# A graph layer with routed experts on one core: smaller late blocks of tokens, their weights copied by ACT, and four places for their buffers

## What is computed

```python
# x: 10000 x 128, adj: 10000 x 10000, float32
h = item_feat @ W_item.T + b_item
x = x + relu(adj @ h + layernorm(x) @ W_user.T + b_user)
xf = layernorm(x)
probs = softmax(xf @ gate_w + gate_b)          # 8 experts
vals, idx = top_k(probs, 2)                    # cw: the two weights of each token
for e in range(8):                             # W1: 128 x 256, W2: 256 x 128
    out += cw[:, e] * (gelu(xf @ W1[e] + b1[e]) @ W2[e] + b2[e])
x = x + out
```

## Time and profile before

| | us |
|---|---|
| median of three runs | 1801.21 (1801.1 to 1806.88) |
| the profiled execution | 1804.49 |
| its span, first to last instruction | 1802.7 |
| busy in it: PE, DVE, ACT, POOL | 1463.0, 1289.1, 1058.1, 822.6 |
| granted TensorE clock, mean | 0.906 of full |

### The profile page before, as it was taken

One profiled execution on the slowest core, in us unless ns is written; L12 is line 12 of the kernel. 1 busy time (PEld: TensorE's weight loads), 2 busy tenths in 40 slices (PEclk: granted clock), 3 DMA queues, 4 the chain that ended last, 5 costly groups with the idle time before them and its releaser, 6 DMA issues. The chain is left out here.

```text
span 1802.7 us, 23294 instructions
## 1 busy us (share of the span) xinstructions
PE 1463.0 (81%) x6505; PEld 1186.0 (66%) x6505; DVE 1289.1 (72%) x2462; ACT 1058.1 (59%) x1227; POOL 822.6 (46%) x507
## 2 busy tenths in 40 slices
PE   7999999999898989889898898989889873544340
PEld 6877777877776768677776777767777652433330
DVE  6988888898787778778787787877888763422220
ACT  5766767676675767567676676766767642322220
POOL 2013221331736346273653736437264465566565
PEclk9999999999999989899999999999999985766665
DMA  9999999998989888898998989989899953222222
GB/s 356 337 326 342 333 321 356 338 352 293 299 269 303 267 284 279 274 304 282 296 301 279 299 281 303 296 288 293 274 311 292 293 165 84 50 37 37 34 25 21
DMA packets 226520, 458.52 MB, mean 254 GB/s; under 512 B 78410, under 2 KB 113335, under 8 KB 226333
## 3 DMA queue, kind: packets, MB, share of 16 engines
q1 hardware_dynamic: 123942, 425.69, 68.5%
q0 software_dynamic: 92144, 27.11, 10.4%
q10 hardware_dynamic: 10390, 5.25, 1.0%
HBM read 429.03 MB, written 31.13 MB: 255 GB/s over the span
## 5 line engine op out<-in xcount | busy, mean ns | idle before, releaser
L681 DVE TENSOR_TENSOR a_lo<-raw,a_hi 128x1000 fp32r<-128x1000 f32 (+1 forms) x800 | 927.1, 1185 | 164.1 <-ACT a_hi L539 157.5
L539 ACT ACTIVATE a_hi<-raw 128x1000 fp32r<-128x1000 f32 (+1 forms) x800 | 812.1, 1027 | 339.8 <-PE acc L950 173.6
L948 PE MATMUL acc<-a_hi,h_hi 128*128 128x500 f32 x1580 | 657.5, 416 | 58.4 <-DVE a_lo L681 42.4
L950 PE MATMUL acc<-a_hi,h_lo 128*128 128x500 f32 x1580 | 624.3, 395 | 0.0
L949 PE MATMUL acc<-a_lo,h_hi 128*128 128x500 f32 x1580 | 624.2, 395 | 0.0
L477 POOL DMA_INDIRECT out<-yr_sb,tok_at x156 | 364.1, 2334 | 380.2 <-DVE yr_sb L851 330.7
L948 PEld LDWEIGHTS acc<-a_hi,h_hi 128*128 128x128 f32 x1580 | 305.6, 193 | 158.2 <-DVE a_lo L681 96.3
L950 PEld LDWEIGHTS acc<-a_hi,h_lo 128*128 128x128 f32 x1580 | 303.9, 192 | 63.1
L949 PEld LDWEIGHTS acc<-a_lo,h_hi 128*128 128x128 f32 x1580 | 306.0, 194 | 55.7 <-issue 4.6
L457 POOL DMA_INDIRECT lists<-rows_sb,dest_at x160 | 238.5, 1490 | 137.5 <-issue 66.9
L444 POOL TENSOR_TENSOR rstd_sb<-var_sb,power_sb 125x4 f32<-125x4 f32 x20 | 38.2, 1909 | 271.7 <-DVE var_sb L704 271.7
(11 more groups left out here) (160 smaller groups left out, 1358.7 us busy)
## 6 DMA issues: line engine op xcount, KB each, us to landing
raw<-in_adj_main SPq DMA_DIRECT2D x780, 500.0 KB, 6.0
xg_sb<-lists SPq DMA_DIRECT2D x39, 273.4 KB
xr_sb<-in_xR SPq DMA_DIRECT2D x20, 250.0 KB
out<-x_sb ACTq DMA_DIRECT2D x20, 250.0 KB
items<-in_itemT SPq DMA_DIRECT2D x13, 384.0 KB, 8.7
lists<-rows_sb,dest_at POOLq DMA_INDIRECT x160
out<-yr_sb,tok_at POOLq DMA_INDIRECT x156, 8.1
lists<-in_filling SPq DMA_DIRECT2D x8, 273.4 KB, 3.9
```

Source lines behind the costliest of these rows:

```text
L539: nc.scalar.activation(a_hi[q][0:rows, 0:cols], raw[s][0:rows, 0:cols], ACT.Copy).then_inc(hi_ready, 1)
L681: nc.vector.tensor_tensor(a_lo[s][0:rows, 0:cols], raw[s][0:rows, 0:cols], val(a_hi[q][0:rows, 0:cols]), ALU.subtract).then_inc(lo_ready, 1)
L948: nc.tensor.matmul(acc[:, 0:T], w_hi, m_hi, start=(k == 0), stop=False)
L950: last = nc.tensor.matmul(acc[:, 0:T], w_lo, m_hi, start=False, stop=(k == KT))
```

## The change

Blocks ahead of the late ones are 31 rather than 30: three (`EARLY`) run beside the tail of the last tile, which is walked over 52 positions rather than 40. Late blocks have 4, 2 or 1 parts of 125 rows, by `late_blocks`: a block may have u parts while the waiting rows are certain to fill it in at least one list. With 4500 rows waiting this gives 4, 4, then seven times 2, then twenty-one times 1, 30 blocks with 43 parts. Row counts in `picked` and in the loads are in rows and not in blocks. Filler is 125 rows rather than 500 for each list. ACT copies the late blocks' weights (`copy_expert`) into one of three places; GpSimd copies only those of the first 31. `picked`, `one_hot` and the scaled rows have four places. GpSimd's order has `tail` ahead of the add of the block before, in every pass. In DVE's late loop pick comes first and the meta last. A few positions in the passes move by one: the second load (19 to 20), `keep` (22 to 23 and 34 to 35), `to_rows` (24 to 25, 36 to 37).

```diff
 PER = 2
 FIRST = 6
+EARLY = 3
 LOOPED = PER * (NB - FIRST)
+NLATE = LOOPED + EARLY
+def full(units):
+    return E * (units * TQ - 1) + 1
-WAITING = 2 * N - T * (LOOPED + PER)
-LATE = E + (WAITING - E) // T
-BLOCKS = LOOPED + PER + LATE
-NLATE = LOOPED + PER
+def late_blocks(waiting):
+    found = []
+    for units in (Q, 2, 1):
+        while waiting >= full(units):
+            found.append(units)
+            waiting -= units * TQ
+    return found + [1] * (E + (waiting - E) // TQ)
+LATE = late_blocks(2 * N - T * NLATE)
+BLOCKS = NLATE + len(LATE)
...
+def w_slot(n):
+    return n % 2 if n < NLATE else (n - NLATE + 1) % 3
...
+        added_rows = [yr_sb, raw[3], raw[6], raw[7]]
+        experts = [(w_block[s][:, 0, :], w_block[s][:, 1, :]) for s in range(2)] + [(a_hi[2][:, 0:WW], a_hi[3][:, 0:WW])]
...
-                sp.dma_start(lists[bass.ds(at, T), :], filling).then_inc(ends_filled, 16)
+                sp.dma_start(lists[bass.ds(at, TQ), :], filling[0:TQ, :]).then_inc(ends_filled, 16)
...
-            for i in range(FIRST, NB + 1):
+            for i in range(FIRST, NB):
                 n = PER * (i - FIRST)
                 weights(n)
+                tail(i)
                 if n:
                     add(n - 1, i - 2)
-                tail(i)
-                if i < NB:
-                    user(i)
+                user(i)
                 weights(n + 1)
                 add(n, i - 1)
                 dispatch(i)
...
             for n in range(NLATE, BLOCKS):
-                if n + 3 < BLOCKS:
-                    weights(n + 3)
                 add(n, NB)
...
+            def copy_expert(n):
+                act.wait_ge(picked_ready, n + 1)
+                at = act.value_load(picked[slot(n)][0:1, 1:2], min_val=0, max_val=E - 1)
+                act.wait_ge(down_done, n + 1 - w_reuse(n))
+                act.wait_ge(y_kept, n + 1 - w_reuse(n))
+                for half in range(2):
+                    nc.scalar.activation(experts[w_slot(n)][half], w_table[:, half, bass.ds(at * WW, WW)], ACT.Copy).then_inc(w_parted, 1)
+                nc.scalar.activation(b_block[w_slot(n)][:, :], bias_sb[:, bass.ds(at * NBIAS, NBIAS)], ACT.Copy).then_inc(w_parted, 1)
...
+            late_pick(NLATE)
+            late_pick(NLATE + 1)
+            for n in range(NLATE - 1, BLOCKS + 2):
+                if NLATE + 2 <= n + 3 < BLOCKS:
+                    late_pick(n + 3)
+                if NLATE <= n + 1 < BLOCKS:
+                    split_rows(numbered(n + 1), work(n + 1), units(n + 1))
+                if NLATE <= n < BLOCKS:
+                    split_g(numbered(n), work(n), units(n))
+                if NLATE <= n - 2 < BLOCKS:
+                    scale(numbered(n - 2), added_rows[yr_slot(n - 2)], slot(n - 2), 16 * units_before(n - 1 - yr_reuse(n - 2)), units(n - 2))
+                if NLATE <= n + 1 < BLOCKS:
+                    read_meta(numbered(n + 1), work(n + 1), slot(n + 1), (n + 1) % 2,
+                              16 * units_before(n + 2 - slot_reuse(n + 1)), units(n + 1))
```

More of the change, by code:

```diff
@@ L63 @@
 CAP = N + T
-SPARE = E * CAP // T
+SPARE = E * CAP
 WW = 2 * H
@@ L322, in build @@
         w_copied = sem("w_copied")
+        w_parted = sem("w_parted")
         meta_step = sem("meta_step")
@@ L426, in _ @@
             for n in range(NLATE, BLOCKS):
-                load_block(numbered(n), n % 2, work(n)["rows"], reuse(n), 16 * 2 * Q * NB)
+                load_block(n, NB)
         @block.gpsimd
@@ L598, in blocks @@
[L598 to L608 removed]
+                nc.scalar.activation(w["y"][:, 0:wide(u)], ps_y[:, 0:wide(u)], ACT.Identity,
+                                     bias=b_block[ws][:, HH:HH + 1]).then_inc(y_kept, 1)
@@ new lines, in blocks @@
+            def blocks(i, p, per):
+                w = works[0]
+                for s in range(per):
+                    at = p - s * APART
+                    if at == B_HI:
+                        split_rows(in_pass(i, s), w, 1, Q)
+                    if at == B_GELU:
+                        gelu(in_pass(i, s), w, 1, s % 2, Q)
+                    if at == B_GHI:
+                        split_g(in_pass(i, s), w, 1, Q)
+                    if at == B_KEEP:
+                        keep(in_pass(i, s), w, 1, s % 2, Q)
@@ L887, in _ @@
                 one_pass(i, True, True)
-            for p in range(NPOS):
+            for p in range(NPOS + APART):
+                blocks(NB, p, EARLY)
                 tail(NB, p)
@@ L1015, in down @@
-            def down(count, w, s):
+                    w_hi, w_lo = (half[:, j * P:(j + 1) * P] for half in expert)
+                    z = ps_z[j][:, 0:wide(u)]
+                    nc.tensor.matmul(z, w_hi, x_hi, start=True, stop=False)
+                    nc.tensor.matmul(z, w_hi, x_lo, start=False, stop=False)
+                    nc.tensor.matmul(z, w_lo, x_hi, start=False, stop=True).then_inc(z_done, 1)
+            def down(count, w, expert, u):
                 since(pe, y_kept, count(1, 0))
+                y = ps_y[:, 0:wide(u)]
```

331 lines of the change are left out of this document (163 added, 168 removed).

## The result

The changed kernel took 1754.03 us (median, 1749.78 to 1756.46) against 1801.15 of the kernel before beside it: a ratio of 0.973, 95% interval 0.9701 to 0.9758. The forecast was 1768, 33 us less; 47 came. The profiled execution has a span of 1751.3 us (before 1802.7), so the two spans differ by 51.4, and they are what the steps are read from.

A forecast was written before the change was run, and what follows sets the result against it. The 250 us end was taken as bound by a chain of adds and landings, not an engine's work. First late add 1562.9 + links 202.5 + end 7.1 - passes 3 = 1769.5 span, 1768 as median; range 1740 to 1790.

The forecast's parts named there:

- The late links: Chain of adds of the late blocks: 202.5 us from first late add to last, against 234.1 + 6.9 before.
- four places take VectorE's 3.1 us out of the link: Late blocks: with four places, VectorE needs only the add of four blocks ago, so its 3.1 us leave the path.
- The small link: Late blocks of one add: landing plus 0.85 us, 5.65 without contention to 6.65 with full, taken as 6.0.
- The passes: Passes 7 to 19, with the tail ahead of the add: 0.2 us gained a pass, 3 us in all.
- that time does not move when PE gets there sooner: Passes 7 to 19: adjacency loads, issued before PE's stall ends on full DMA engines, set ACT's time up to 1349.73.
- Rival 1: Passes 7 to 19: PE's stall counts, 13 x 3 = 39 us more gained, 1729 us; chance 0.14.
- From load to first late add: Filling before the late adds: three turns of the in-order loop stay, 26.9 us as before.
- Its bound, 3 less: Start of the late blocks: up to 3 us less where GpSimd's weight copies, 1.9 us each, sat in the filling.
- The scatter: Last tile: power about 6.7 us earlier, block 28's add 6.2 earlier, but scatter after block 29's adds; first late load 8.4 later.
- ring of a small block: Late small blocks: compute hand-overs bind, not the landing; 7.3 us a block, 26 us more, 1794 us; chance 0.14.
- The slower case: Late small blocks: ACT's weight copying overlaps nothing, 8.7 us a block, 54 us more, 1822 us; chance 0.05.

## Why the prediction was right, and where its steps failed

The forecast of faster was right, and the time was in the range, 14 us below the number. Step by step:

**The late links: right in number by luck, wrong in cause.** 202.5 us forecast, 198.2 and 197.7 measured, with links of 12.7, 8.1 and 5.8 us for 12.7, 8.15 and 6.0. The step that failed is the sentence that four places take VectorE's 3.1 us out of the link. Two places of scaled rows cost nothing, while the order on VectorE alone, put into the kernel before, took 1.6 us out of each link in the mean and 25.5 us out of the time. The number survived because the changed kernel also moves that call, and the link of a landing and 0.85 us holds whatever removes VectorE from it. The small link was taken 0.2 too high: 5.8 was measured in the mean and 5.7 in the median, where the lower end of the earlier trace rows gives 4.8 + 0.85 = 5.65. That end held, load or no load beside it.

The Trainium skill, page "DMA: Bandwidth & Descriptors", section "Anatomy of one DMA — SWDGE (gpsimd) path", has a fixed part per transfer that size does not touch, and I had noted that it speaks against cutting blocks. The runs agree in kind, with 3.45 us for a block here in place of the page's 2.0 for a transfer: cutting sixteen blocks into thirty gave 5 us of chain, and going back to seventeen of other sizes gave 38. In the prediction I let that warning stand without pricing the list that it asks for.

**The passes: 0.2 us forecast, 1.0 to 1.3 measured.** The step that failed is "that time does not move when PE gets there sooner". It moved, by 1.3 of 3.3 us of stall in one pair of traces and by 1.0 of 4.5 between before and after; whether through the stall or through the adds' later place was not separated. Rival 1 with its 3 us a pass was further off on the other side.

**From load to first late add: 26.9 taken, 21.6 measured.** "Three turns of the in-order loop, which stay": they stay, but before, the third block waited for a weight copy that waited for the first block's `y`. I had written that the copy's going gains nothing, since it was hidden; hidden it was in the links, not in the filling. Its bound, 3 less, was in the prediction, for the wrong reason (the copy's own 1.9 us), and too small.

**The scatter: +9.7 measured, +8.3 forecast.** The power came 3.8 us after the relu instead of 11.0, as forecast, but block 28's add gained 3.6 us of it and not 6.2 (27.0 us after the relu, 30.6 before); by the rows its `y` is kept 5.0 us earlier (21.7 after the relu, 26.6 before), and VectorE scales it 3.6 earlier (26.0 and 29.6), behind the places of the tile's rows and the next block's work in its queue. No run tried that queue. Block 29's adds came 40.1 us after the relu, 1.2 later than forecast, and the scatter 1.4.

**The rivals.** Neither ring of a small block bound: of GpSimd's 21 waits in the small blocks one ends with VectorE's scaling, and moving the copies to another engine changed nothing. The slower case, ScalarE's copying in series, did not occur; its two copies took 1.15 us and the register read 0.28, with 0.15 of register work behind it, where 1.2 and 0.6 had been taken.

## What to carry to other kernels

Where a wait for a buffer stands in an in-order queue, look first at what stands behind it in that queue: moving one call behind the work that the critical engine needs gave about half of what this change brings, and the same wait in another place ate nearly the whole gain of an earlier scatter. Before work is cut into smaller pieces, measure the cost of a piece as a fixed part and a part per size, and fit the list of sizes to that price; filling in a large piece can be cheaper than a small piece that is always full. A stall that "comes back later" may come back only in part, so it wants a price and not a zero, and a price of a few us wants more than one pair of traces.

## What the runs showed of the hardware

A chain of blocks of accumulating indirect transfers, each block waiting for the landing of the one before, cost 3.45 us a block and 2.30 us a transfer, for one to four transfers, and this hardly changed with the load beside it. In 1600 to 1650 us TensorE was granted 0.50 of its clock in the changed kernel, the 1.2 GHz level, where the mean was 0.66 before, though its busy time was a little higher (22.5 us against 21.6 in 50), in more and smaller instructions (100 against 73). It did not lengthen the chain: in the small blocks no wait of GpSimd ended with TensorE.
